# A top-2 FFN's rows loaded seven tiles ahead instead of five, one scatter issued ahead of the last batch's sends, and the last additions of three batches made by Pool

## The chip, the cores and the metric

One core of a Trainium2 chip runs the whole program. The metric is the device time in microseconds (us) of one execution; the runs shown are three, and their median counts. A change of under about 0.5% of this kernel's time (some 10 us) can't be told from none.

## What is computed

Two transformer layers over x of 8 batches x 512 tokens x 128 features, float32. Each layer is an adaLN attention and an adaLN FFN. The change lies wholly in the last of the four, the FFN of layer 1, a mixture of 8 experts of which every token uses two:

```python
xf = x.reshape(B * S, D)                       # D = 128, E = 8 experts, P = 512 hidden
scores = xf @ Wr + br
_, top_idx = jax.lax.top_k(scores, 2)
mask = jax.nn.one_hot(top_idx, E).sum(-2) > 0
router_weights = softmax(where(mask, scores, -inf))
h = gelu(einsum('td,edp->etp', xf, W1) + b1[:, None, :])
y = einsum('etp,epd->etd', h, W2) + b2[:, None, :]
out = einsum('te,etd->td', router_weights, y)
x = x + gb * out
```

## The kernel before

A list of steps (`order.steps`) is written out by hand, and every engine walks the same list, each doing its own share of a step; semaphores tie the shares together. The list ends with the routing of the last batch (b = 7) interleaved with the first seven FFN tiles. After the list each engine has a plain loop for what is left.

**Routing.** For each batch the router chooses two experts a token. DVE works out at which row of a DRAM array `sent` each of the token's two copies goes (`dest`, L2080), and Pool sends them: eight indirect DMAs of 128 rows a batch (step `send`, L2250, semaphore `d_sent`). DVE also makes a list of tiles: tile t2 is 256 rows (`SLOTS`) of one expert. There are 39 tiles (`TILES`). The first 14 (`EARLY`) can be listed before the last batch is routed.

**One tile.** SP loads the expert's weights, a pack of 578 KB (`load_pack`, L1051, three buffers, `PACKS`), and the tile's 256 rows, 132 KB (`load_rows`, L1060, eight buffers `got`, `SENT`). TensorE transposes the rows (`turn2`, L1096), DVE copies them out of PSUM (`rows_T`, L1667), TensorE multiplies up (`up2`), ACT applies gelu (L1500), TensorE multiplies down (`down2`; both at the helper's line L1090), DVE adds the bias (L1675, `y2_drained`) and multiplies by the router weight (L1682, `y2_ready`), and Pool scatters the 256 results to their tokens' rows of the DRAM array `y_rows` with two indirect DMAs (`scatter`, L2134, semaphore `d_y`). TensorE's order in tile t is turn2(t+2), up2(t+1), down2(t).

**SP's order around the change.** SP issues all its DMAs in one order, and a wait holds up what is behind it. Before the loop it loads three packs and `AHEAD` tiles of rows. Then iteration t2 does load_pack(t2+3), which waits until DVE has drained tile t2, and load_rows(t2+`AHEAD`). The latter reads its row number first and then waits for

```python
w.wait_ge(d_y[t2 % SENT], 16 * SLOTS // P * (t2 // SENT))     # L1059
```

that is, until the scatter of the tile eight before has landed, because the scatter reads its destinations from the same `got` buffer. With `AHEAD` = 5 iteration t waits for scatter(t-3).

**Pool's order around the change.** Pool too works in one order: the routing's `stat` of the last batch, scatter(0), (1), (2), (3), (4), the eight sends of the last batch, and then, in its own loop, scatter(5) to (38).

**The end.** When all scatters have landed, SP and ACT load for each batch the two halves of its result into `both` (L1077, L1656, 256 KB each, `d_both`). DVE then does three operations a batch, all 128x512 float32 with both inputs in SBUF: add the halves (L2113), multiply by the gain (L2116), add x (L2119, `out_ready`). SP stores batch after batch, in order of b (L1081), and waits for the stores to land (L1083).

Of the kernel before, what the change touches and what calls it, by code (L numbers as in the profile page):

```python
# [16 lines left out]
ALU = mybir.AluOpType  # L17
# [3 lines left out]
P = 128  # L21
B, S, D = 8, 512, 128
NT = S // P
# [43 lines left out]
TILES_OF = B * S // SLOTS  # L67
ROW = D + 4
PACK = 2 * F + FC + D
PACKS, SENT, AHEAD = 3, 8, 5  # L70


EARLY, FRONT = 14, 7
# [125 lines left out]
def build(nc, t, out):  # L199
    ctx = ExitStack()  # L200
    with ctx:
# [155 lines left out]
        x_tokens = leave([B, NT, D])  # L357
        gain = leave([B, D])
# [31 lines left out]
        both = carve([B, 2, NT, D])  # L390
# [92 lines left out]
        turn_of, back1_of, hrow_of, rank_of, gains_of, fold_of = {}, {}, {}, {}, {}, {}  # L483
# [123 lines left out]
        for b in range(B):  # L607
            n = b * NU
# [281 lines left out]
        def tile(t2):  # L890
            return lambda: add("tile", t2=t2)

        def scatter(t2):
            return lambda: add("scatter", t2=t2)

        for f in (lambda: add("first_tile"), lambda: back1(B - 1), tile(0), lambda: finish1(B - 1), tile(1), tokens_f,
                  stat_f, scatter(0), tile(2), center_f, norm_f, tile(3), router_f, second_f, hrow_f, tile(4), chosen_f,
                  weights_f, scatter(1), scatter(2), tile(5), rank_f, place_f, row_f, scatter(3), scatter(4), tile(6),
                  send_f):
            f()  # L900
        scattered = order.count["scatter"]
# [19 lines left out]
        d_y = [semaphore(f"d_y{z}") for z in range(SENT)]  # L921
        d_both = [semaphore(f"d_both{b}") for b in range(B)]
        tables_ready, row_ready, tiles_ready = (semaphore(n) for n in ("tables_ready", "row_ready", "tiles_ready"))
        turn2_full, got_ready, up2_full, hid2_done, down2_full, y2_drained, y2_ready, out_ready = (
            semaphore(n) for n in ("turn2_full", "got_ready", "up2_full", "hid2_done", "down2_full", "y2_drained",
                                   "y2_ready", "out_ready"))
        meet = semaphore("meet")

        mod_exp, silu_ready, mod_full, mod_ready, consts_ready = (
# [2 lines left out]
        aux_full, aux_drained, pool_done, dve_chain = (  # L932
            semaphore(n) for n in ("aux_full", "aux_drained", "pool_done", "dve_chain"))
# [36 lines left out]
        def drained(s):  # L970

            return s.aux + 1

        with nc.Block() as block:

            @block.sync
            def _(sp):
                w = Waits(sp)
# [13 lines left out]
                for s in order.steps:  # L992
# [19 lines left out]
                    elif s.kind == "copy_out":  # L1012
                        b, a = s["b"], s["a"]
# [3 lines left out]
                    elif s.kind == "parts_out":  # L1017
                        b, what = s["b"], s["what"]
# [4 lines left out]
                    elif s.kind == "stack":  # L1023
                        b, what, r = s["b"], s["what"], s["r"]
# [11 lines left out]
                    elif s.kind == "qload":  # L1036
                        a, q = s["a"], s["q"]
                        b, g = divmod(a, NG)
# [38 lines left out]
                    sp.dma_start(both[:, b, 0, :, :], y_dram[b * S:(b + 1) * S, :].rearrange(  # L1077
                        "(n p) d -> p n d", p=P)).then_inc(d_both[b], 16)
                for b in range(B):
                    w.wait_ge(out_ready, b + 1)  # L1080
                    sp.dma_start(out_v[:, b * NT:(b + 1) * NT, :], both[:, b, 0, :, :]).then_inc(d_out[b], 16)  # L1081
                for b in range(B):
                    sp.wait_ge(d_out[b], 16)  # L1083
# [576 lines left out]
            def _(dve):  # L1660
                w = Waits(dve)
                chain = Chain(w, dve_chain)
# [65 lines left out]
                for s in order.steps:  # L1728
# [13 lines left out]
                    elif k == "mod_first":  # L1742
                        n = SC_A * B
# [4 lines left out]
                    elif k == "mod_signs":  # L1748
                        n = GA_A * B
# [21 lines left out]
                    elif k == "stat":  # L1771
                        L, which, b = s["L"], s["which"], s["b"]
# [12 lines left out]
                    elif k == "center":  # L1785
                        L, which, b = s["L"], s["which"], s["b"]
# [26 lines left out]
                    elif k == "scores":  # L1813
                        u = s["u"]
                        i, n = u["i"], u["n"]
# [6 lines left out]
                    elif k == "maxima":  # L1822
                        n = s["u"]["n"]
# [4 lines left out]
                    elif k == "late":  # L1828
                        n = s["u"]["n"]
                        w.wait_ge(ctx_drained, n + 1)  # L1830
                        dve.reciprocal(ctx_sum[:, 0, n % 2, 2 * P:CW], ctx_sum[:, 0, n % 2, 2 * P:CW]).then_inc(recip, 1)  # L1831
                    elif k == "out_proj":
                        b, i = s["b"], s["i"]
# [4 lines left out]
                    elif k == "router0":  # L1838
                        b = s["b"]
# [65 lines left out]
                    elif k == "before_gather":  # L1905
                        b = s["b"]
# [9 lines left out]
                    elif k == "gather":  # L1916
                        b = s["b"]
# [29 lines left out]
                    elif k == "back" and s["x"] == E - 1:  # L1947
                        b = s["b"]
# [17 lines left out]
                    elif k == "scores1" and s["u"]["i"]:  # L1966
                        u = s["u"]
                        i, n = u["i"], u["n"]
# [139 lines left out]
                for t2 in range(FRONT, TILES):  # L2108
                    tile(t2)
                for b in range(B):  # L2110
                    w.wait_ge(aux_drained, drained(gains_of[b // 4]))
                    w.wait_ge(d_both[b], 32)
                    chain.mark(dve.tensor_tensor(both[:, b, 0, :, :], both[:, b, 0, :, :], both[:, b, 1, :, :],  # L2113
                                                 ALU.add))
                    chain.wait()
                    chain.mark(dve.tensor_tensor(both[:, b, 0, :, :], both[:, b, 0, :, :],  # L2116
                                                 gain[:, b, :].unsqueeze(1).to_broadcast([P, NT, D]), ALU.mult))
                    chain.wait()
                    dve.tensor_tensor(both[:, b, 0, :, :], both[:, b, 0, :, :], x_tokens[:, b, :, :],  # L2119
                                      ALU.add).then_inc(out_ready, 1)  # L2120

            @block.gpsimd
            def _(pool):
# [6 lines left out]
                def scatter(t2):  # L2130
                    z = t2 % SENT
                    w.wait_ge(y2_ready, t2 + 1)
                    for h in range(SLOTS // P):
                        pool.indirect_dma_start(  # L2134
                            y_dram, bass.IndirectOffsetOnAxis(ap=got[:, z, h, D:D + 1].bitcast(U32), axis=0),
                            y_out[:, z, h, :], None, bounds_check=2 * B * S - 1, oob_is_err=False).then_inc(
                                d_y[z], 16)
# [116 lines left out]

                for t2 in range(scattered, TILES):
                    scatter(t2)


# [34 lines left out]
```

## Time and profile before

| what | value |
|---|---|
| three runs | 2068.82, 2073.63, 2080.97 us; median 2073.63 us |
| profiled execution, its own time | 2066.3 us |
| its span | 2064.2 us |
| mean granted TensorE clock | 0.957 |
| TensorE busy | 1803.1 us (87%) |
| DVE / ACT / Pool busy | 1145.4 / 690.3 / 743.9 us |

All times below are microseconds from the start of the span of the profiled execution. The FFN of layer 1 is the stretch from about 1854 to the end; the last batch's routing ends at about 1896, the last tile at 2036, and what is after that is the end described above. "Remote" in a row is a wait whose releaser the profile does not tell. A line of the timeline gives the start, the duration, the engine, line and operation, what it writes and reads, how many instructions are merged, and in brackets the engine's idle time before it with what ended it. SPq rows are DMA issues.

### The profile page before, as it was taken

Reading aid. Unit: us, or ns where it says so; the run is one execution under the profiler, and the core shown is the slowest. Engines: PE = TensorE matmul, PEld = TensorE weight load, DVE = VectorE, ACT = ScalarE, POOL = GpSimd, SP = SyncE. Lnnn points to the kernel's source line nnn. Section 1 sums busy time; section 2 is a strip of 40 time slices with the busy share of each in tenths; the row PEclk is TensorE's granted clock in tenths of the full one; section 3 lists DMA queues with packets and bytes.
Section 4 is the critical chain, followed back from the end, with each engine's and each line's share of the span. In section 5 each row is a group of like instructions: output and inputs, shape, how many; then the busy total and the mean of one; then the engine's idle time right before and its main releaser. Section 6 shows DMA issues by size and latency. Waiting matters only on the chain.

```text
span 2064.2 us, 76401 instructions
## 1 busy us (share of the span) xinstructions
PE 1803.1 (87%) x34864; PEld 1320.1 (64%) x34864; DVE 1145.4 (55%) x2282; ACT 690.3 (33%) x1041; POOL 743.9 (36%) x727
## 2 busy tenths in 40 slices
PE   6899999999888888899999898978888887977994
PEld 4666766766666666575524666766666666756883
DVE  4656666566666665674265555645565545544224
ACT  2333434334333333333101342323333332323431
POOL 2464655555545551311030323313132232014442
PEclk9999999999999999999998999999999989989997
DMA  9500000000000000300012313222131313024666
GB/s 310 164 2 2 2 2 2 2 2 2 2 2 2 2 2 2 103 1 1 3 31 46 82 29 82 52 56 68 38 78 38 73 34 79 20 62 130 198 206 185
DMA packets 81042, 113.45 MB, mean 55 GB/s; under 512 B 9486, under 2 KB 63506, under 8 KB 80289
## 3 DMA queue, kind: packets, MB, share of 16 engines
q1 hardware_dynamic: 71376, 97.16, 17.6%
q0 software_dynamic: 4544, 8.54, 1.2%
q8 instruction: 273, 4.47, 0.9%
q10 hardware_dynamic: 4800, 2.89, 0.6%
q14 instruction: 49, 0.39, 0.1%
HBM read 83.25 MB, written 45.68 MB: 62 GB/s over the span
## 4 chain that ended last, share of the span: by engine, by line
PE 50%; DVE 13%; issue 6%; ACT 2%; DMA 1%; POOL 1%; another core or an unknown queue 1%; POOLq 0%; DVEq 0%; SPq 0%; ACTq 0%
PE psum L1090 47%; DVE colmax L1819 2%; DVE colmax L1972 2%; DVE ctx_sum L1831 1%; PE psum L1438 1%; DVE rowmax L1980 1%; DMA arena<-in_pack 1%; ACT arena L1575 1%; DVE rowmax L1826 1%; DVE arena L1792 1%; DVE stats L1779 1%; DVE raw L1807 1%; PE psum L1165 1%; PE psum L1157 1%
## 5 line engine op out<-in xcount | busy, mean ns | idle before, releaser
L1090 PE MATMUL psum<-arena 128*32 128x32 f32 (+9 forms) x10680 | 679.2, 256 | 84.2 <-issue 56.9
L1090 PEld LDWEIGHTS psum<-arena 128*32 128x32 f32 (+4 forms) x10680 | 489.2, 127 | 205.0 <-issue 128.4
L1575 ACT ACTIVATE arena<-psum 128x1024 f32<-128x1024 f32 (+1 forms) x192 | 169.4, 882 | 359.3 <-PE psum L1090 291.7
L1090 PE MATMUL psum<-prob,ffw 128*32 128x128 f32 x5120 | 206.4, 280 | 40.4 <-DVE rowmax L1826 37.6
L1090 PE MATMUL psum<-neg_ident,rowmax 128*32 128x128 bf16 (+3 forms) x4352 | 215.9, 252 | 11.4 <-issue 10.3
L1972 DVE TENSOR_REDUCE colmax<-psum 128x256 bf16<-128x768 f32 (+2 forms) x160 | 178.3, 1114 | 82.4 <-PE psum L1090 59.3
L1819 DVE TENSOR_REDUCE colmax<-psum 128x512 bf16<-128x2048 f32 (+2 forms) x96 | 168.4, 1755 | 74.7 <-PE psum L1090 74.6
L1980 DVE TENSOR_REDUCE rowmax<-psum 128x2 bf16<-128x256 f32 (+1 forms) x192 | 98.0, 510 | 189.9 <-PE psum L1090 181.3
L1590 ACT COPY ctx_sum<-psum 128x384 f32<-128x384 f32 x128 | 61.2, 478 | 412.4 <-PE psum L1090 366.1
L1090 PEld LDWEIGHTS psum<-prob,ffw 128*32 128x32 f32 x5120 | 139.6, 112 | 71.7 <-DVE rowmax L1826 60.1
L2209 POOL TENSOR_TENSOR arena<-ctx_sum 128x256 f32<-128x256 f32 x128 | 95.4, 745 | 243.9 <-DVE ctx_sum L1831 233.2
L1090 PEld LDWEIGHTS psum<-neg_ident,rowmax 128*32 128x32 bf16 (+1 forms) x4352 | 139.7, 99 | 51.3 <-issue 39.7
L1558 ACT ACTIVATE prob<-psum 128x2048 f32<-128x2048 f32 (+3 forms) x128 | 158.5, 1238 | 29.2 <-PE psum L1090 28.5
L1831 DVE RECIPROCAL ctx_sum<-ctx_sum 128x128 f32<-128x128 f32 x128 | 120.4, 941 | 80.0 <-ACT ctx_sum L1590 79.8
L2158 POOL TENSOR_TENSOR rope_a<-raw,arena 128x512 f32<-128x512 f32 x86 | 110.1, 1280 | 118.8 <-ACT raw L1538 110.6
L2250 POOL DMA_INDIRECT sent<-ffw x64 | 62.6, 978 | 218.4 <-DVE ffw L2087 201.3
L2160 POOL TENSOR_TENSOR rope_b<-raw,arena 128x512 f32<-128x512 f32 x96 | 126.7, 1320 | 37.2 <-ACT raw L1538 29.9
L1090 PE MATMUL psum<-ident_bf,colmax 128*128 128x128 bf16 x1024 | 113.0, 224 | 24.4 <-DVE colmax L1972 17.4
L1090 PEld LDWEIGHTS psum<-ident_bf,colmax 128*128 128x128 bf16 x1024 | 75.5, 100 | 89.4 <-issue 31.1
L2148 POOL TENSOR_SCALAR moments<-moments 128x4 f32<-128x4 f32 x32 | 8.4, 263 | 341.5 <-DVE moments L1783 340.9
L1090 PE MATMUL psum<-prob,ones_col 128*32 128x128 f32 x2560 | 130.8, 277 | 0.0
L1090 PE MATMUL psum<-causal,ident_bf 128*128 128x256 bf16 (+1 forms) x448 | 113.1, 299 | 7.3 <-ACT arena L1575 6.3
(260 smaller groups left out, 2530.3 us busy)
## 6 DMA issues: line engine op xcount, KB each, us to landing
arena<-in_pack SPq DMA_DIRECT2D x39, 578.0 KB
sent<-in_empty SPq DMA_DIRECT2D x9, 2112.0 KB, 34.7
arena<-qk_parts SPq DMA_DIRECT2D x96, 128.0 KB
q_copies<-arena SPq DMA_DIRECT2D x32, 256.0 KB, 3.9
prob<-q_copies SPq DMA_DIRECT2D x128, 64.0 KB, 3.6
qk_parts<-arena SPq DMA_DIRECT2D x16, 384.0 KB, 3.8
arena<-sent SPq DMA_DIRECT2D x39, 132.0 KB
ffw<-in_L_w SPq DMA_DIRECT2D x1, 2048.0 KB, 9.0
```

The costliest lines, as they stand in the source:

```text
L1090: return pe.matmul(o, lhsT, rhs, start=start, stop=stop, skip_group_check=True)
L1558: act.activation(prob_of(u).rearrange("p z j c -> p z (j c)"), scores_of(u).rearrange("p z j c -> p z (j c)"), ACT.Exp, scale=HD0 ** -0.5) ...
L1575: act.activation(probs_of(i)[:, :, h0 * P:(h0 + nh) * P], slot(n)[:, 0:(i + 1) * W].rearrange("p (j c) -> p j c", c=W), ACT.Exp, scale=HD1 ...
L1590: act.copy(ctx_sum[:, 0, n % 2, 0:CW], psum[:, CTX, 0:CW]).then_inc(ctx_drained, 1)
L1819: dve.tensor_reduce(colmax[:, n % 2, :].rearrange("p (z c) -> p z c", z=2), scores_of(u).rearrange("p z j c -> p z c j"), AX.X, ALU.max).t ...
L1831: dve.reciprocal(ctx_sum[:, 0, n % 2, 2 * P:CW], ctx_sum[:, 0, n % 2, 2 * P:CW]).then_inc(recip, 1)
L1972: dve.tensor_reduce(colmax[:, n % 2, 0:W], slot(n)[:, 0:(i + 1) * W].rearrange("p (j c) -> p c j", c=W), AX.X, ALU.max).then_inc(colmax1_d ...
L1980: dve.tensor_reduce(rowmax[:, n % 2, 0:nh], psum[:, MAX, 0:nh * P].rearrange("p (h k) -> p h k", k=P), AX.X, ALU.max).then_inc(max_done, 1)
L2158: chain.mark(pool.tensor_tensor(rope_a[:, z, :], raw[:, z, :], table[:, 0, :], ALU.mult))
L2160: chain.mark(pool.tensor_tensor(rope_b[:, z, :], raw[:, z, :], table[:, 1, :], ALU.mult))
L2209: chain.mark(pool.tensor_tensor(ctxT[b % 2][:, 2 * q:2 * q + 2, i * P:(i + 1) * P], ctx_sum[:, 0, n % 2, 0:2 * P].rearrange("p (c q) -> p ...
L2250: pool.indirect_dma_start(sent, bass.IndirectOffsetOnAxis(ap=dest[:, b % 2, h, n:n + 1], axis=0), sent_row[:, b % 2, h, n, :], None).then_ ...
```

## The change

`AHEAD` becomes 7, the step scatter(5) is put into the list ahead of tile(6) and the last batch's sends, and a new list `BY_POOL` names the batches whose three last operations Pool makes after its last scatter; DVE skips these. `out_ready` becomes two semaphores, and SP waits for the one of the batch's engine.

```diff
-PACKS, SENT, AHEAD = 3, 8, 5
+PACKS, SENT, AHEAD = 3, 8, 7
+BY_POOL = (1, 4, 6)
...
-                  weights_f, scatter(1), scatter(2), tile(5), rank_f, place_f, row_f, scatter(3), scatter(4), tile(6),
+                  weights_f, scatter(1), scatter(2), tile(5), rank_f, place_f, row_f, scatter(3), scatter(4), scatter(5), tile(6),
                   send_f):
...
+        out_ready = [semaphore(n) for n in ("out_by_dve", "out_by_pool")]
...
                 for b in range(B):
-                    w.wait_ge(out_ready, b + 1)
+                    w.wait_ge(out_ready[b in BY_POOL], 1 + sum((c in BY_POOL) == (b in BY_POOL) for c in range(b)))
                     sp.dma_start(out_v[:, b * NT:(b + 1) * NT, :], both[:, b, 0, :, :]).then_inc(d_out[b], 16)
...
                 for b in range(B):                                  # DVE
+                    if b in BY_POOL:
+                        continue
...
                 for t2 in range(scattered, TILES):                  # Pool
                     scatter(t2)
+                for b in BY_POOL:
+                    w.wait_ge(aux_drained, drained(gains_of[b // 4]))
+                    w.wait_ge(d_both[b], 32)
+                    chain.wait()
+                    chain.mark(pool.tensor_tensor(both[:, b, 0, :, :], both[:, b, 0, :, :], both[:, b, 1, :, :],
+                                                  ALU.add))
+                    chain.wait()
+                    chain.mark(pool.tensor_tensor(both[:, b, 0, :, :], both[:, b, 0, :, :],
+                                                  gain[:, b, :].unsqueeze(1).to_broadcast([P, NT, D]), ALU.mult))
+                    chain.wait()
+                    pool.tensor_tensor(both[:, b, 0, :, :], both[:, b, 0, :, :], x_tokens[:, b, :, :],
+                                       ALU.add).then_inc(out_ready[1], 1)
```

## Rows read from the trace of the kernel before

**Rows 1.** Busy time by stretch: busy (instructions) an engine, then TensorE's clock, DMA share, GB/s.
```profile
1950.00:2000.00 50.00, 47.10 (x314) 42.57 (x313) 14.84 (x48) 19.70 (x48) 23.31 (x24) 1.00 0.64 200
2030.00:2064.00 34.00, 4.77 (x38) 4.45 (x36) 17.86 (x30) 1.64 (x4) 5.82 (x6) 0.63 0.71 186
```
**Rows 2.** Chain of waits in order of time, from tile 7 on: start, us, what.
```profile
1897.07 9.88 another core or an unknown queue
...
2025.37 3.80 DMA arena<-in_pack
...
2038.56 2.10 DMA y_rows<-arena
```
**Rows 3.** Timeline, first tiles: SP's issues and TensorE's tile 4.
```profile
1868.12 0.38 SPq L1060 DMA_DIRECT2D arena<-sent  x1
...
1871.80 0.35 SPq L1051 DMA_DIRECT2D arena<-in_pack  x1
...
1880.15 0.35 SPq L1051 DMA_DIRECT2D arena<-in_pack  x1
...
1881.35 3.68 PE L1090 MATMUL psum<-arena 128*128 128x256 f32 x24
```
**Rows 4.** Timeline of Pool, first tiles, the last sends and what follows.
```profile
1872.37 0.98 POOL L2134 DMA_INDIRECT y_rows<-arena  x1 [0.30 <-DVE arena L1682]
...
1892.81 0.96 POOL L2250 DMA_INDIRECT sent<-ffw  x1 [3.78 <-DVE ffw L2087]
...
1902.93 0.99 POOL L2134 DMA_INDIRECT y_rows<-arena  x1 [0.30 <-issue]
```
**Rows 5.** Timeline of DVE, ACT and SP before and in the long wait after tile 7.
```profile
1889.29 0.48 DVE L1682 TENSOR_SCALAR arena<-arena 128x128 f32<-128x128 f32 x2
1891.85 0.17 DVE L2087 TENSOR_SCALAR ffw<-ffw 128x8 uint32<-128x8 f32 x1
...
1906.97 0.42 DVE L1675 TENSOR_TENSOR arena<-psum,arena 128x256 f32<-128x256 f32 x1 [9.91 <-remote]
1912.71 3.11 ACT L1500 ACTIVATE arena<-psum,arena 128x256 f32<-128x256 f32 x8 [13.66 <-remote]
```
**Rows 6.** Timeline of a steady tile: Pool's second scatter, SP's rows.
```profile
1940.22 0.97 POOL L2134 DMA_INDIRECT y_rows<-arena  x1 [0.31 <-issue]
1943.55 0.38 SPq L1060 DMA_DIRECT2D arena<-sent  x1
```
**Rows 7.** Times to landing of the end's loads (L1077), then of its stores (L1081).
```profile
L1077 SPq DMA_DIRECT2D arena<-y_rows x8: 383/562/1796, 2040.8 to 2046.6; - x8
DMA to landing us min/median/max: 3.5/8.3/10.7
...
L1081 SPq DMA_DIRECT2D out<-arena x8: 372/1666/1958, 2048.4 to 2061.4; - x8
DMA to landing us min/median/max: 2.3/6.1/9.6
```
**Rows 8.** Timeline of the end: the first batch and the last operation of DVE.
```profile
2044.82 0.69 DVE L2113 TENSOR_TENSOR arena<-arena 128x512 f32<-128x512 f32 x1 [9.00 <-DMA arena<-y_rows]
2046.88 0.69 DVE L2113 TENSOR_TENSOR arena<-arena 128x512 f32<-128x512 f32 x1
...
2060.65 0.69 DVE L2119 TENSOR_TENSOR arena<-arena,ffw 128x512 f32<-128x512 f32 x1
```
**Rows 9.** Timeline of DVE and Pool near the start: 128x512 operations side by side.
```profile
15.30 0.69 DVE L1801 TENSOR_TENSOR rope_a<-raw,arena 128x512 f32<-128x512 f32 x1 [4.46 <-ACT raw L1538]
15.33 1.78 POOL L2160 TENSOR_TENSOR rope_b<-raw,arena 128x512 f32<-128x512 f32 x1 [8.58 <-ACT raw L1538]
...
17.95 1.26 POOL L2171 TENSOR_TENSOR arena<-rope_a,raw 128x512 f32<-128x512 f32 x1 [0.84 <-DVE raw L1807]
17.98 1.79 DVE L1801 TENSOR_TENSOR rope_a<-raw,arena 128x512 f32<-128x512 f32 x1
```
**Rows 10.** Groups of Pool's instructions: count, busy us, mean ns of one.
```profile
L2174 POOL TENSOR_TENSOR arena<-rope_a,raw 128x512 f32<-128x512 f32 x32 | 40.9, 1278 | 42.4 <-DVE raw L1807 42.0
```

More of the change, by code:

```diff
@@ L923, in build @@
         tables_ready, row_ready, tiles_ready = (semaphore(n) for n in ("tables_ready", "row_ready", "tiles_ready"))
-        turn2_full, got_ready, up2_full, hid2_done, down2_full, y2_drained, y2_ready, out_ready = (
+        turn2_full, got_ready, up2_full, hid2_done, down2_full, y2_drained, y2_ready = (
             semaphore(n) for n in ("turn2_full", "got_ready", "up2_full", "hid2_done", "down2_full", "y2_drained",
-                                   "y2_ready", "out_ready"))
+                                   "y2_ready"))
+        out_ready = [semaphore(n) for n in ("out_by_dve", "out_by_pool")]
         meet = semaphore("meet")
@@ L2119, in _ @@
                     dve.tensor_tensor(both[:, b, 0, :, :], both[:, b, 0, :, :], x_tokens[:, b, :, :],
-                                      ALU.add).then_inc(out_ready, 1)
+                                      ALU.add).then_inc(out_ready[0], 1)
             @block.gpsimd
```

## The prediction

> **What bounds the kernel now.** I read the page's busy shares first (TensorE 87%, so everything before the last tiles is TensorE's), then the busy time by stretch, the chain of waits over the last 200 us, the timelines of SP and Pool, and last the end alone. Nothing of the change acts before about 1847, so only three stretches count.
>
> From 1950 on the tiles run steadily: TensorE is busy 47.10 of 50 us while the DMA engines are at 0.64 [rows 1]; a pack takes 3.80 from issue to landing [rows 2], which with TensorE's 3.7 us a tile makes 4.2 us a tile. In the middle lies a hole. After tile 7, while Pool issues the last batch's eight sends and right behind them the scatters held up by these, the chain stands 9.88 us on something it can't name [rows 2]; DVE waits 9.91 us for TensorE's result of tile 7, and ACT 13.66 [rows 5]. After the last tile, from 2041 on, TensorE has nothing left, and the end belongs to DVE and the DMA engines: DVE's 24 operations take it from 2044.82 to 2061.34 [rows 8], 2.06 us a batch (2046.88 less 2044.82), and the last store lands 2.3 us after its issue [rows 7].
>
> **Rows seven tiles ahead.** No DMA is added; 39 row loads stay, each issued two iterations earlier. What changes is the wait in front of each: iteration t now wants scatter(t-1) landed instead of scatter(t-3). Behind this wait on SP stands the next pack, and TensorE waits for that.
>
> In the steady part: Pool's second scatter of tile 14 is issued at 1940.22, and SP comes to the next row load at 1943.55 [rows 6]. A scatter lands 2.10 us after its last issue [rows 2], here at 1942.3: 1.2 us before it is wanted. Cost nothing; if one lands later, SP has some 2.7 us until the next pack is due, so even a scatter 2 us late is hidden. Nor is there a gain: the chain shows packs, never rows, and TensorE's one wait on SP's loads is for packs.
>
> At the start it is different, because scatter(0) stands behind the routing's `stat` on Pool and its second half is issued only at 1872.37 [rows 4]. SP will come to load_rows(8) at 1868.12 [rows 3] and stand until 1872.37 + 2.10 = 1874.5. Behind it is load_pack(5), which was issued at 1871.80; now it goes at 1874.5 + 1.1 (as SP needs between two issues) = 1875.6, 3.8 us late, and lands 3.80 later, at 1879.4. It is needed by tile 4's up2(5), which starts at 1881.35 [rows 3] for other reasons (the router's steps). Cover left: 1.9 us. load_rows(9) then waits for scatter(1), about 1877, and load_pack(6), due at 1880.15 [rows 3], is not touched. I take 0, bounds 0 and +1.5 (scatters and pack landing 3.4 us later than reckoned, as they share the DMA engines), and not below 0, since nothing comes sooner that anyone waits for. Were the cover gone, the whole 3.8 would show. The two extra loads before the loop find SP idle until 1862. The last two iterations have no row load beside the pack; the last pack without one beside it took the 3.80 that I use, so I give nothing for that.
>
> **One scatter ahead of the sends.** Without it, load_rows(13) in iteration 6 would stand until scatter(5), issued from 1902.93 on [rows 4], had landed; with it, it doesn't. y_out of tile 5 ends at 1889.29 + 0.48 = 1889.77 [rows 5]; Pool sees it 0.8 us later, and two issues of 0.98 with 0.3 between end at 1892.8. The sends were ready at 1892.81 [rows 4] (their destinations and weights done at 1891.85 + 0.17 [rows 5]), and now go at 1893.1: +0.3 us on eight sends. Nobody waits for these but load_rows(14), not due before 1908.
>
> What it does to the hole is the least certain term. The hole lasts as long as Pool issues without a pause: eight sends and scatters 5 and 6, twelve DMAs of 1.27 us, from 1892.81 to 1907.8, and DVE gets TensorE's result at 1906.97 [rows 4, 5]. Now the unbroken run starts with scatter(5) at 1890.5 and ends one pair (2 x 1.27 = 2.5 us) sooner, at 1905.5. If the release follows the run's end, 2.5 us come back at most; if it follows how many issues have gone by since the run began, TensorE is held from its first instruction of tile 7, up to 2.3 us sooner than before, and tile 8 is pushed by up to 2. And even a release at 1904.5 must be followed by pack 10, which is issued when tile 7 is drained and needs 3.80. Bounds -2.5 and +2; I take 0, in the middle, since no row favours an end.
>
> **Pool makes three batches.** This removes nine operations from DVE (9 x 0.69) and puts nine on Pool. What counts is whether the two engines can work side by side. The rows of the start show the same two shapes: Pool's 128x512 with two SBUF inputs takes 1.26 to 1.28 alone [rows 9, 10]; started 0.03 behind a DVE operation of the same kind it takes 1.78, and a DVE operation started 0.03 behind Pool's takes 1.79 instead of 0.69 [rows 9]. So they run one after the other: a pair costs 17.98 + 1.79 - 17.95 = 1.82 us whoever is first, instead of 1.27 side by side.
>
> Work out the end with that. DVE does b = 0 alone until 2046.96. Half of `both` for b = 1 is in by then, and from there on Pool has nine operations and DVE twelve: nine pairs x 1.82 = 16.4, three of DVE alone x 0.685 = 2.05, together 18.4, so 2046.96 + 18.4 = 2065.4 against 2061.34: +4.1 us. Data doesn't hold this up much: the last load is issued at 2046.6 and lands within 10.7, at 2057.3 [rows 7], while the pairs are still behind. The last store then follows as before (2.3 us).
>
> Bounds: with no interference at all, Pool would do b = 1, 4, 6 by about 2060.4 and DVE end at 2059.5, but the stores also have to drain: they were issued from 2048.4 on and the first landed 9.6 us later [rows 7], at 2058, since loads at a DMA share of 0.71 over the whole stretch [rows 1] go first; eight stores from there leave little. So -0.5 at best. At worst Pool's operations cost 10% more with a broadcast gain, and Pool's chain lags: +6. I take +4.1, by the row of the same shape.
>
> The Trainium skill, "SBUF — State Buffer", section "SBUF: two separate sides", speaks against this part: a DVE instruction with two SBUF inputs and a Pool instruction that reads SBUF take one shared port pair as an exclusive lock, the first for the whole instruction, and the other fully blocks. By that rule nothing of an operation overlaps: 9 x 1.27 + 12 x 0.69 = 19.7 from 2046.96, an end at 2066.7, +5.4. The rows show a pair at 1.82 where the rule would have 1.96, so a little does overlap; the measured pair decides.
>
> **Sum.** On the profiled execution: 2066.3 + 0 (rows) + 0 (hole) + 4.1 (end) = 2070.4. The median of the three runs is 7.3 above the profiled one, a spread of the executions that the change doesn't touch, so 2073.63 + 4.1 = 2077.7.
>
> **Rivals.**
> 1. Faster: the hole closes. Place: between tile 7 and tile 9; price: the pair that leaves the unbroken run, -2.5, and the end gains its -0.5 because the stores' draining sets it: 2073.63 - 3 = 2070.6 (2063.3 on the profiled one). For it: DVE's release at 1906.97 falls at the last of the run's issues. Against: the pair of [rows 9] for the end, pack 10 for the hole. It decides if Pool's operations of the end show 1.27 beside DVE's.
> 2. SP's new wait bites. load_rows(8) is released late, pack 5 lands after 1881.35, tile 4 waits 1.5, and the router's steps of the last batch, which stand behind tile 4, with it; the sooner throttled tile 7 adds 2. 2073.63 + 4.1 + 3.5 = 2081.2. For it: the cover is a mere 1.9 us in a stretch where packs, rows and scatters meet. Against: all of it must be late together.
> 3. The change of engines is hidden: the pairs cost 1.82, but the stores' draining and the loads' landing set the end (the b = 7 loads land at 2057.3 and three operations and eight stores follow), so that only +1 is seen: 2074.6. Against: DVE's pairs are 8 us behind the last landing.
>
> **Chances.** Forecast 0.55, rival 1 0.18, rival 2 0.15, rival 3 0.12. The terms together run from -3 to +9.5, thus 2070.6 to 2083.1; the three runs lie from 4.8 below to 7.4 above their median, and half of that goes on either end: 2068 to 2086. Slower by over 0.5% (10.4 us) needs rival 2 with all bounds and a high draw: 0.11. Faster by over 0.5% needs more than any term holds: 0.05. The rest, 0.84, is within 0.5%, which is about what a measurement of this kernel can tell from no change.
>
> **What would show it.** In the end stretch: Pool's nine operations at about 1.8 and DVE's mostly at 1.2 to 1.8 instead of 0.69, the last DVE operation near 2065. On SP: load_rows(8) at about 1874.5 and load_pack(5) at 1875.6, with tile 4 starting when it did. On Pool: scatter(5) at 1890.5, sends from 1893.1. In the hole: tile 7 drained at 1905 to 1909. Wrong would be: operations of 0.69 and 1.27 side by side (then the end gains), a TensorE wait for pack 5, or tile 7 drained before 1903.

## The result, and the profile after

Eighteen runs of each kernel, taken in turn: before 2069.57 us median (2060.61 to 2081.59), changed 2076.12 us (2070.28 to 2085.57), ratio 1.0034 with a 95% interval of 1.0017 to 1.0050. So the change costs 7 us (3.5 to 10.3), or 0.34%: little, but with eighteen runs of each the interval lies clear of 1. 2077.7 had been forecast from a median of 2073.63, that is +4.1.

The profiled execution of the changed kernel took 2085.57 us (span 2083.8), 19 us more than that of before. That is no measure of the change: DVE takes the FFN's tile 0 out of PSUM at 1874.1 instead of 1861.8, and in a second profile of the same changed kernel at 1864.5. All comparisons below are therefore of stretches, measured from that point ("+13.0" is 13.0 us after it; the tiles in the table are counted at the same operation of theirs) or from the first operation of the end.

| stretch, us | before | changed | changed, second profile |
|---|---|---|---|
| tile 0 to tile 6 | 34.0 | 35.0 | 37.5 |
| tile 6 to 7 | 11.15 | 10.77 | 8.74 |
| tile 7 to 9 | 10.2 | 11.3 | 8.2 |
| tile 0 to the last tile | 173.0 | 174.2 | 173.5 |
| end: DVE's first operation to its last | 16.52 | 19.60 | 19.61 |
| end: DVE's first operation to the program's end | 19.34 | 25.25 | 25.26 |

The middle moved by about 1 us, which is no more than two executions differ by: from tile 0 to the last took 175.4 in an experiment below ("One batch on Pool") whose middle is that of before. The end is 5.9 us longer in both profiles.

First the steady part and the end by stretches (columns as in [rows 1]): TensorE 47.67 us of 50, DMA share 0.65, as before; in the end Pool is now as busy as DVE.

```profile
1965.00:2015.00 50.00, 47.67 (x315) 42.88 (x315) 14.88 (x48) 19.70 (x48) 23.31 (x24) 1.00 0.65 199
2045.00:2083.80 38.80, 3.34 (x30) 3.15 (x29) 19.19 (x21) 0.65 (x2) 19.35 (x15) 0.61 0.62 163
```

The end on DVE, timeline, to be held against [rows 8]. L2118, L2121 and L2124 are the three operations of a batch:

```profile
2058.51 0.69 DVE L2118 TENSOR_TENSOR arena<-arena 128x512 f32<-128x512 f32 x1 [9.11 <-DMA arena<-y_rows]
...
2062.62 1.05 DVE L2118 TENSOR_TENSOR arena<-arena 128x512 f32<-128x512 f32 x1 [1.96 <-DMA arena<-y_rows]
...
2068.36 1.63 DVE L2124 TENSOR_TENSOR arena<-arena,ffw 128x512 f32<-128x512 f32 x1
2069.92 1.74 DVE L2118 TENSOR_TENSOR arena<-arena 128x512 f32<-128x512 f32 x1
2071.70 1.63 DVE L2121 TENSOR_TENSOR arena<-arena,ffw 128x512 f32<-128x512 f32 x1
2073.36 1.63 DVE L2124 TENSOR_TENSOR arena<-arena,ffw 128x512 f32<-128x512 f32 x1
2074.92 1.74 DVE L2118 TENSOR_TENSOR arena<-arena 128x512 f32<-128x512 f32 x1
2076.70 0.69 DVE L2121 TENSOR_TENSOR arena<-arena,ffw 128x512 f32<-128x512 f32 x1
2077.42 0.69 DVE L2124 TENSOR_TENSOR arena<-arena,ffw 128x512 f32<-128x512 f32 x1
```

And the same stretch on Pool:

```profile
2061.85 1.26 POOL L2269 TENSOR_TENSOR arena<-arena,ffw 128x512 f32<-128x512 f32 x1
...
2069.53 1.59 POOL L2272 TENSOR_TENSOR arena<-arena,ffw 128x512 f32<-128x512 f32 x1
2071.08 1.70 POOL L2266 TENSOR_TENSOR arena<-arena 128x512 f32<-128x512 f32 x1
...
2074.53 1.59 POOL L2272 TENSOR_TENSOR arena<-arena,ffw 128x512 f32<-128x512 f32 x1
```

Where Pool is idle, DVE's operation takes 0.69; beside Pool's it takes 1.63 to 1.74, and Pool's 1.59 instead of 1.26. From 2069.92 to 2074.92 three pairs pass: 1.67 us a pair. Of DVE's last twelve operations seven are such full pairs. This is the turn-taking of [rows 9]. DVE's sum: nine operations fewer, -6.2 (9 x 0.685); waiting for batch 2's data, to which it comes sooner since it skips batch 1, +2.0, so that the three operations of batch 1 (2.06) are no gain at all; its last twelve operations in 15.5 us (2062.62 to 2078.11) instead of 8.2, +7.3. Together +3.1.

The other 2.8 us are not on DVE. The last store is issued at 2078.14 and lands 2.3 us later, at 2080.4; the program should end at 2080.7. It ends at 2083.8. What stands there is on the line that closes the program, where each engine waits for its own work to come to an end (DRAIN). The rows of that line, of the changed kernel (engine, operation, duration in ns, start in us):

```profile
L977 POOLq DRAIN  x1: 8740/8740/8740, 2074.5 to 2074.5; - x1
L977 DVEq DRAIN  x1: 725/725/725, 2077.4 to 2077.4; - x1
...
L977 SPq DRAIN  x1: 13/13/13, 2080.7 to 2080.7; - x1
L977 SPq EVENT_SEMAPHORE  x1: 17/17/17, 2083.7 to 2083.7; - x1
```

and of the kernel before:

```profile
L974 POOLq DRAIN  x1: 9740/9740/9740, 2036.9 to 2036.9; - x1
...
L974 SPq DRAIN  x1: 13/13/13, 2063.9 to 2063.9; - x1
```

Pool's closing wait lasts until 7.1 us after Pool's last operation: 2074.5 + 8.74 = 2083.2 against 2076.12 now, 2036.9 + 9.74 = 2046.6 against 2039.5 before. Before, it was over 17 us ahead of SP. Now Pool's last operation comes 4.3 us before the last store lands, and SP, done at 2080.7, stands 3.0 us for it.

The start of the FFN, on SP (L1063 rows, L1054 pack), to be held against [rows 3]:

```profile
1887.09 0.38 SPq L1063 DMA_DIRECT2D arena<-sent  x1
1888.23 0.35 SPq L1054 DMA_DIRECT2D arena<-in_pack  x1
```

and on TensorE, tile 4:

```profile
1893.56 3.68 PE L1093 MATMUL psum<-arena 128*128 128x256 f32 x24
```

load_rows(8) stands until scatter(0) has landed, at +13.0, and pack 5 is issued at +14.1 (12.7 and 13.8 were forecast). Tile 4 starts at +19.5, as in [rows 3] (1881.35 less 1861.8 is 19.55): hidden.

On Pool, scatter(5), the first send, and scatters 6 and 7, to be held against [rows 4]:

```profile
1902.77 0.97 POOL L2139 DMA_INDIRECT y_rows<-arena  x1 [1.54 <-DVE arena L1685]
...
1905.33 0.96 POOL L2255 DMA_INDIRECT sent<-ffw  x1 [0.30 <-issue]
...
1916.80 0.99 POOL L2139 DMA_INDIRECT y_rows<-arena  x1 [0.30 <-issue]
1921.61 0.97 POOL L2139 DMA_INDIRECT y_rows<-arena  x1 [3.82 <-DVE arena L1685]
```

Scatter(5) goes at +28.7 and the first send at +31.2, both as forecast. The unbroken run now ends at 1917.8 (+43.7), not at +46.0 as in [rows 4]. And the hole is still there; chain of waits, then DVE's row, to be held against [rows 2] and [rows 5]:

```profile
1911.30 8.57 another core or an unknown queue
1919.89 0.43 DVE arena L1678
1920.49 3.84 DMA arena<-in_pack
```

```profile
1919.89 0.42 DVE L1678 TENSOR_TENSOR arena<-psum,arena 128x256 f32<-128x256 f32 x1 [8.20 <-remote]
```

Tile 7 is released at +45.8 (before +45.2), though the run ended 2.3 us sooner. In the six profiles that have the hole the release comes anywhere from 0.8 us before the run's end (the kernel before) to 2.3 us after it, and 2.2 after it in "One batch on Pool", whose scatters and sends stand as before; so it does not follow the run's end. Behind it pack 10 takes its 3.84.

### The profile page after: what moved, and what is told of

It reads as the page before. It is cut to its first block, busy times and chain, and to the rows that moved or that the text cites. A ratio compares the mean times of both kernels' runs of the same rounds, so it can differ in the third digit from the quotient of the medians.

```text
span 2083.8 us, 76402 instructions
## 1 busy us (share of the span) xinstructions
PE 1814.8 (87%) x34864; PEld 1329.9 (64%) x34864; DVE 1146.1 (55%) x2273; ACT 690.5 (33%) x1041; POOL 757.8 (36%) x736
## 4 chain that ended last, share of the span: by engine, by line
PE 49%; DVE 14%; issue 7%; DMA 2%; ACT 2%; POOL 1%; another core or an unknown queue 1%; SPq 0%; ACTq 0%; DVEq 0%; POOLq 0%
PE psum L1093 47%; DVE colmax L1975 2%; DVE colmax L1822 2%; DMA arena<-in_pack 1%; DVE ctx_sum L1834 1%; PE psum L1441 1%; DVE rowmax L1983 1%; DVE raw L1810 1%; ACT arena L1578 1%; DVE rowmax L1829 1%; DVE arena L1795 1%; PE psum L1168 1%; ACT prob L1561 1%; PE psum L1160 1%
## 5 line engine op out<-in xcount | busy, mean ns | idle before, releaser
L1093 PE MATMUL psum<-prob,ffw 128*32 128x128 f32 x5120 | 211.9, 285 | 39.9 <-DVE rowmax L1829 37.3
L1093 PEld LDWEIGHTS psum<-prob,ffw 128*32 128x32 f32 x5120 | 143.8, 114 | 71.9 <-DVE rowmax L1829 59.5
L1561 ACT ACTIVATE prob<-psum 128x2048 f32<-128x2048 f32 (+3 forms) x128 | 158.5, 1238 | 28.7 <-PE psum L1093 28.1
L1093 PE MATMUL psum<-ident_bf,colmax 128*128 128x128 bf16 x1024 | 112.9, 223 | 28.1 <-DVE colmax L1975 19.5
```

Of the source, the lines that this page charges most:

```text
L1093: return pe.matmul(o, lhsT, rhs, start=start, stop=stop, skip_group_check=True)
L1561: act.activation(prob_of(u).rearrange("p z j c -> p z (j c)"), scores_of(u).rearrange("p z j c -> p z (j c)"), ACT.Exp, scale=HD0 ** -0.5) ...
```

## The experiments

Theory A, after this reading: the end costs +3.1 by turn-taking and +2.8 by Pool's closing wait, and the middle nothing. Rivals: the closing wait is only a symptom of the end (B); SP's new wait costs something in the middle (C).

The kernels below were timed in three sets, each beside its own runs of before. In set 1 (the end alone, the middle alone, something late on Pool, Pool busy) before took 1992.31 us (23 runs, 1985.94 to 2002.4); in set 3 (rows six ahead again, the first two batches, the two with scatters held) 1995.83 us (29 runs, 1985.46 to 2009.89). No profile of these two sets has the hole, and the mean granted clock is about 0.97. Set 2 (the whole again, rows alone, rows six ahead, one batch) was like the forecast's runs: before 2070.78 us (19 runs, 2065.29 to 2082.4), clock 0.955, and the hole in every profile. The expectations speak of a chip with or without the hole. But the chip number noted with set 1 is 10, and with sets 2 and 3 it is 13 both times; so whether the hole goes with the chip or with something that changes in time is open, and only "a set with the hole" and "a set without" can be said. This matters more than most edits.

**The end alone.** The changed kernel with the two middle edits undone.

```diff
-PACKS, SENT, AHEAD = 3, 8, 7
+PACKS, SENT, AHEAD = 3, 8, 5
...
-                  ..., scatter(3), scatter(4), scatter(5), tile(6),
+                  ..., scatter(3), scatter(4), tile(6),
```

> Only the end of the change: Pool makes the last operations of batches 1, 4 and 6; rows five tiles ahead and the scatters as before. The end stretch is read from DVE's first operation of the end to the end of the span: 19.4 us in the kernel before, 25.3 in the changed one. Theory (the end alone makes the kernel slower, in two parts: DVE and Pool take turns, 3.1 us, and Pool's closing drain outlasts all else by 2.9): 25.3 again, a median 5 to 7 us above before. Rival (the middle makes half of it): the end stretch is 25.3 too, as a profile shows it, but the median only some 3 us above before.

Measured: 2000.63 us (12 runs), ratio 1.0038 (1.0021 to 1.0056), that is +7.6 us (4.2 to 11.2), where 5 to 7 were expected. DVE's end 19.60 and end stretch 25.25, to 0.01 those of the changed kernel. So the end alone is enough for the loss of the changed kernel.

**The middle alone.** The kernel before with the two middle edits.

```diff
-PACKS, SENT, AHEAD = 3, 8, 5
+PACKS, SENT, AHEAD = 3, 8, 7
...
-                  ..., scatter(3), scatter(4), tile(6),
+                  ..., scatter(3), scatter(4), scatter(5), tile(6),
```

> Only the middle of the change: rows seven tiles ahead and scatter(5) ahead of the last sends; DVE makes all of the end. The middle is read from tile 0's drain to tile 38's (DVE's bias additions): 173.0 us before, 174.3 in the changed kernel. Theory: 173 to 174.5, end stretch 19.4, a median within 2 us of before. Rival (the middle costs the measured surplus over the predicted 4.1): a median 3 or more above before. Rival from the prediction (the hole closes): 170.5 or less, a median below before.

Measured: 1998.48 us (12 runs), ratio 1.0029 (1.0011 to 1.0046), +5.8 us (2.2 to 9.2), where 2 at most was expected. The rival's "3 or more" came, but from a place that neither had named. End stretch 19.34, the old one. SP's timeline:

```profile
1832.20 0.35 SPq L1051 DMA_DIRECT2D arena<-in_pack  x1
1838.58 0.38 SPq L1060 DMA_DIRECT2D arena<-sent  x1
1839.72 0.35 SPq L1051 DMA_DIRECT2D arena<-in_pack  x1
```

Pool's, from the last send to scatter(6):

```profile
1833.59 0.96 POOL L2250 DMA_INDIRECT sent<-ffw  x1 [0.30 <-issue]
1834.86 0.99 POOL L2134 DMA_INDIRECT y_rows<-arena  x1 [0.30 <-issue]
1836.15 0.99 POOL L2134 DMA_INDIRECT y_rows<-arena  x1 [0.30 <-issue]
```

and TensorE's:

```profile
1843.64 5.28 PE L1090 MATMUL psum<-arena 128*128 128x256 f32 x24 [3.22 <-DMA arena<-in_pack]
```

load_rows(14) wants scatter(6), whose issues stand behind all eight sends and end at 1837.1. Until 1838.58 SP stands; pack 11, due at about 1836.1 (tile 8 is drained at 1835.5), goes only at 1839.72, and TensorE waits 3.22 for it. Tile 9 to 10 takes 8.72 us; in the kernels of sets 1 and 3 without this wait it takes 3.7 to 4.2. The 4.6 to 5.0 us more are the wait and a slower block behind it (5.28 instead of 3.78 us, at a granted clock of 0.76 from 1843 to 1850). From tile 0 to the last 167.9 us pass, in those others 161.7 to 164.0. Theory C holds here, at another load than the one that I had watched. Where the hole is, load_rows(14) comes late anyway, because the hole keeps SP back, and the same wait is free.

**Something late on Pool.** The kernel before; Pool's last operation is a memset of 128x4 after DVE's last.

```diff
                 for t2 in range(scattered, TILES):
                     scatter(t2)
+                w.wait_ge(out_ready, B)
+                pool.memset(minus_half[:, :], -0.5)
```

> The kernel before, with one tiny memset (128x4) on Pool that waits until DVE has made its last operation; nothing else is changed, and no operation of Pool's stands beside DVE's. Theory (Pool's closing drain ends 7.1 us after Pool's last operation, whatever that is, and is hidden only while Pool finishes early): the end stretch grows from 19.4 to about 24 us (last DVE operation 16.5 after the first, the memset, 7.1, half a microsecond). Rival (the drain of the changed kernel took long because of the big operations or of the port): it stays within 0.5 us of 19.4.

Measured: 2002.33 us (one run), DVE's end 16.57, end stretch 24.06 against 19.3. Pool's timeline and the closing line:

```profile
1992.89 0.10 POOL L2258 MEMSET minus_half<- 128x4 f32 x1 [21.84 <-DVE arena L2119]
```

```profile
L974 POOLq DRAIN  x1: 7220/7220/7220, 1992.9 to 1992.9; - x1
...
L974 SPq DRAIN  x1: 13/13/13, 1995.4 to 1995.4; - x1
```

One operation of 0.10 us, put late on Pool, costs 4.7 us: SP is done at 1995.4 and the program ends at 2000.3. B would have the stretch stay at 19.3; it is out.

**Pool busy without SBUF inputs.** The kernel before; Pool makes three memsets of 128x1024 for each of three batches in place of operations that read.

```diff
+                for b in (1, 4, 6):
+                    w.wait_ge(d_both[b], 32)
+                    for _ in range(3):
+                        chain.wait()
+                        chain.mark(pool.memset(rope_a[:, :, :].rearrange("p z c -> p (z c)"), 0.0))
```

> The kernel before, with nine memsets of 128x1024 on Pool into a dead buffer, three each when the data of batches 1, 4 and 6 have landed; they write SBUF and read none of it. DVE still makes all 24 operations. Theory (the turns are taken over the read side that a two-input DVE operation and a reading Pool operation share): DVE's operations stay at 0.69 us and its 24 end 16.5 us after the first, end stretch 19.4. Rival (any work of Pool's in SBUF holds DVE up): DVE operations beside a memset take 1 us or more, and the 24 end 19 us or later after the first.

Measured: 1995.85 us (one run). DVE's operations keep their 0.69 beside Pool's 2.97 us of memsets a batch, and its end is 16.66 (16.5 before). So that Pool is busy in SBUF is not enough to make DVE wait. That it is Pool's reading which does it fits this, but a memset differs from an addition in more than that, and no run puts another kind of reading operation on Pool there. The end stretch is 21.68, where 19.4 was expected, since Pool's last memset comes late and the closing wait with it:

```profile
1983.71 2.97 POOL L2261 MEMSET rope_a<- 128x1024 f32 x3 [0.64 <-DMA arena<-y_rows]
```

```profile
L974 POOLq DRAIN  x1: 8083/8083/8083, 1985.7 to 1985.7; - x1
```

(1985.7 + 8.08 = 1993.8, 7.1 after 1986.7.)

**The whole change again**, as it stands in the diff, in set 2.

> The changed kernel itself, once more. Between tile 7 and tile 9 the profile before has a hole of some 9 us in which TensorE's results reach nobody (tile 7 drained 11.2 us after tile 6, tile 8 another 5.9), and the profiles of the experiment with the end alone have none (4.2 and 4.6). Theory (SP's new wait costs what the hole does not hide): where a run has no hole, load_rows(14) stands until scatter(6) has landed, 3 us or more, pack 11 is that late, and the whole costs 10 to 13 us; where it has the hole, load_rows(14) waits for nothing and the whole costs 6 to 7. Rival (the middle costs a fixed share, whatever the hole does): the same loss either way.

Measured: 2075.05 us (10 runs), ratio 1.0019 (0.9999 to 1.0040), +3.9 (-0.2 to 8.3). Its profile is the last column of the table: the end is the same to 0.01, the middle within 0.5 us of before. The interval includes 1, so by itself this timing neither repeats the loss nor contradicts it. The other half of the expectation, 10 to 13 us where there is no hole, was not tested: the whole change never ran in such a set. The two parts measured alone in set 1, +7.6 and +5.8, would add up to 13 if neither hides the other.

**Rows alone**, without the moved scatter.

```diff
-PACKS, SENT, AHEAD = 3, 8, 5
+PACKS, SENT, AHEAD = 3, 8, 7
```

> Rows seven tiles ahead and nothing else; scatter(5) stays behind the last batch's sends. Theory: SP stands one iteration earlier, load_rows(13) until scatter(5) has landed, some 12.5 us after the first send, and packs 10 and 11 are late: tile 0's drain to tile 38's at least 3 us longer than with the scatter ahead (167.9 there), where the run has no hole. Rival (the scatter ahead buys nothing): the same 167.9 within 1.

Measured: 2072.57 us (one run). SP in the hole:

```profile
1911.89 0.38 SPq L1060 DMA_DIRECT2D arena<-sent  x1
1915.18 0.00 SPq L1051 DMA_DIRECT2D arena<-in_pack  x1
```

load_rows(13) now stands until scatter(5), behind the sends, has landed (+45.0), and pack 10 goes at +48.3, 2.2 us later after tile 7's drain (+45.5) than in the other kernels (0.6). From tile 7 to 9 11.8 us pass, from tile 0 to the last 173.9; the changed kernel has 11.3 and 174.2, so nothing is seen of the scatter here. The expectation, 3 us more without it, was for a set without the hole and stays untested: what the moved scatter is worth no run shows. SP was free again at +46.1, so its wait for the scatter alone does not account for the pack at +48.3.

**Rows six ahead**, with the moved scatter and the old end.

```diff
-PACKS, SENT, AHEAD = 3, 8, 5
+PACKS, SENT, AHEAD = 3, 8, 6
...
-                  ..., scatter(3), scatter(4), tile(6),
+                  ..., scatter(3), scatter(4), scatter(5), tile(6),
```

> The middle of the change with rows six tiles ahead instead of seven; scatter(5) ahead of the sends; DVE makes all of the end. Iteration t then waits for scatter(t-2). Theory (it is the wait of iteration 7 for scatter(6), which stands behind the eight sends on Pool): load_rows(14) now is issued in iteration 8, pack 11 goes within 0.7 us after tile 8's drain, and tile 0's drain to tile 38's is within 1.5 us of the 161.7 to 163.4 of a middle left as it was. Rival (the scatter ahead of the sends, or any rows loaded early, costs the 4 to 6 us): 166 or more again.

Measured: 2067.03 us (10 runs), ratio 0.9983 (0.9960 to 1.0005). Pack 11 goes 0.6 us after tile 8's drain, as expected, but the 161.7 to 163.4 of the expectation are of a set without the hole, and this set has it: 174.3 us from tile 0 to the last, against 173.0 before, 174.2 in the changed kernel and 175.4 with one batch on Pool. So the profile shows no gain in the middle.

> The version with rows six tiles ahead and the one scatter more, and the old end: timed once more, in more rounds, whether it is below the kernel before at all. From its first timing 0.998 (0.996 to 1.0005). If the one tile less takes SP's wait out of packs' way on every chip, 0.998 to 1.000; if the steps gained there were chance, 1.000 +- 0.001. On a chip without the hole, rows_six waits for scatter(6) one iteration later than rows seven ahead, so tile 9 to 10 keeps its 4.2 us instead of 8.7.

Measured again, in set 3, without the hole: 1991.77 us (12 runs) against 1995.83, ratio 0.9987 (0.9967 to 1.0008). Pack 11 again goes 0.6 us after tile 8's drain, tile 9 to 10 takes 3.74, and tile 0 to the last 162.2, so one iteration less ahead takes SP's wait out of the pack's way. Both intervals hold 1: this version lies below the kernel before in both sets, and is not shown to be faster.

**One batch on Pool**, b = 1 alone, with the middle of before.

```diff
-BY_POOL = (1, 4, 6)
+BY_POOL = (1,)
```

> Pool makes the last operations of batch 1 alone; everything else as before. Pool is done by some 7 us after DVE's first operation of the end, so its 7.1 us of closing drain are over 5 us before the stores. Theory (two separate prices: taking turns about 1.0 a batch, the drain only if Pool finishes last): DVE's operations take 17.3 to 17.6 us from the first to the end of the last, end stretch 20.1 to 20.4. Rival (the whole surplus of 5.9 is in proportion to the batches): 21.3. Rival (one batch less on DVE is a gain when the drain is hidden): below 19.3.

Measured: 2073.35 us (one run). DVE's end 17.85 (+1.3), end stretch 20.66; both lie 0.25 above what was expected. Pool's closing wait starts at 2055.2 and lasts 8.74, over at 2063.9, 7 us before SP is done: hidden. DVE comes to batch 2 before its data:

```profile
2054.78 0.97 DVE L2118 TENSOR_TENSOR arena<-arena 128x512 f32<-128x512 f32 x1 [2.06 <-DMA arena<-y_rows]
2055.78 1.63 DVE L2121 TENSOR_TENSOR arena<-arena,ffw 128x512 f32<-128x512 f32 x1
```

Three operations fewer save 2.06, this wait takes the 2.06 back, and the two lengthened operations add 1.2: that is the +1.3.

**The first two batches on Pool**, with the middle of before.

```diff
-BY_POOL = (1, 4, 6)
+BY_POOL = (0, 1)
```

> The kernel before with the first two batches of the end made by Pool instead of three spread ones. Two parts of the end are told apart. If the engines take turns (a pair 1.67 us), DVE's eighteen operations and Pool's six make 6 x 1.67 + 12 x 0.69 = 18.3 us for the end's additions, +1.8 over the 16.5 of before; and since Pool's last operation then ends some 7 us before DVE's, its closing wait (7.1 us after its last operation) is hidden: end stretch 18.3 + 2.9 = 21.2, +1.9 in all, ratio 1.0009. If the closing wait instead hangs on the program's end and not on Pool's last operation, the stretch is 24 to 25. If only the number of batches mattered, two of the changed kernel's three would cost 2/3 of +5.9, that is +3.9 (stretch 23.2).

Measured: 2001.15 us (10 runs), ratio 1.0009 (0.9983 to 1.0036). The line that closes the program:

```profile
L977 POOLq DRAIN  x1: 8742/8742/8742, 1987.1 to 1987.1; - x1
...
L977 SPq DRAIN  x1: 13/13/13, 2001.5 to 2001.5; - x1
```

The closing wait is over at 1995.8, 5.7 us before SP, whose end now follows DVE's last operation (1998.9) by the usual 2.8. Measured from the first operation of the end, which is Pool's at 1979.76, the additions take 19.15 and the stretch 21.9; 18.3 and 21.2 were expected, without DVE's wait until batch 2's data are in at 1983.42. By then all but the last 0.3 us of Pool's first three operations are over, so the full pairs are three and not six. Six operations on Pool, and no closing cost: it hangs on when Pool's last operation comes, not on their number nor on the program's end. The medians lie 5.3 us apart, but the interval holds 1, and the profile has 2.6 us of it.

**Scatters 5 and 6 held until tile 7 is weighted**, in the kernel before, to see whether the hole's end follows the end of Pool's run.

```diff
-                    w.wait_ge(y2_ready, t2 + 1)
+                    w.wait_ge(y2_ready, 8 if t2 in (5, 6) else t2 + 1)
```

> The kernel before, with scatters 5 and 6 waiting until DVE has weighted tile 7, so that Pool's unbroken run is the eight sends alone (8 x 1.27 = 10.1 us instead of 15). Where the hole between tiles 7 and 9 exists (span above 2050): if the late news of TensorE's work is released when Pool's run ends, DVE gets tile 7 some 4 to 5 us sooner than the 1906.97 of before (measured from tile 0: 40 to 41 instead of 45.1), tile 9 follows sooner by as much, and the time falls by 3 to 5 us, ratio 0.998. If it is released by something that doesn't depend on the run's end (TensorE's clock, the DMA engines' load), tile 7 stays at 45 after tile 0 and the ratio is 1.000 +- 0.001. On a chip without the hole (about 1992) both expect 1.000. The end is the old one: DVE 16.5 us, end stretch 19.3.

Measured: 1994.07 us (10 runs), ratio 0.9995 (0.9973 to 1.0017), in a set without the hole, where both theories had 1.000. It tells nothing about the hole.

**The same with rows six ahead and the moved scatter.**

> Rows loaded six tiles ahead, scatter(5) ahead of the last batch's sends and waiting, as scatter 6, until tile 7 is weighted: this puts scatter(5)'s wait in front of the sends, so the eight sends go only after tile 7. If the hole is made by the sends' unbroken run, tile 7 itself is drained without it (on a chip with the hole: 6 to 7 takes 4 to 5 us instead of 11), and the stall moves behind it, to tiles 8 and 9, where the batch's destinations are wanted much later; the stretch from tile 0 to the last tile then stays at 172 to 175. If the hole belongs to tile 7 for another reason (its clock), 6 to 7 stays at 10 to 11.

Measured: 2008.3 us (one run), 12 us above the median of before, though runs of before in this set reach 2009.89; what counts is the profile. Having no hole, it answers another question, what SP's wait costs at its worst. Pool's last send and scatter(6):

```profile
1851.34 0.96 POOL L2250 DMA_INDIRECT sent<-ffw  x1 [0.30 <-issue]
1852.60 0.98 POOL L2134 DMA_INDIRECT y_rows<-arena  x1 [0.30 <-issue]
1853.89 0.99 POOL L2134 DMA_INDIRECT y_rows<-arena  x1 [0.30 <-issue]
```

SP:

```profile
1844.77 0.35 SPq L1051 DMA_DIRECT2D arena<-in_pack  x1
1856.32 0.38 SPq L1060 DMA_DIRECT2D arena<-sent  x1
1857.46 0.35 SPq L1051 DMA_DIRECT2D arena<-in_pack  x1
```

and TensorE:

```profile
1849.54 5.46 PE L1090 MATMUL psum<-arena 128*128 128x256 f32 x24 [3.02 <-DMA arena<-in_pack]
...
1861.52 6.35 PE L1090 MATMUL psum<-arena 128*128 128x256 f32 x24 [6.30 <-DMA arena<-in_pack]
```

load_rows(14) stands until scatter(6) has landed, and pack 12 behind it, due at about 1846.9 (tile 9 is drained at 1846.3), goes at 1857.46, 10.6 us late. Pack 11 is late too, by 1.6 us, behind load_rows(13) and the held scatter(5). TensorE waits 3.02 and 6.30 for the two and afterwards runs blocks of 3.8 us in 5.46 and 6.35, at a granted clock of 0.68 from 1850 to 1855 and 0.77 from 1855 to 1870. Tile 0 to the last takes 173.8 against 162 to 164.

## Why the prediction was right, step by step

**Rows, 0: right, with its times to 0.3 us.** load_rows(8) at +13.0, pack 5 at +14.1, tile 4 untouched. But the sentence that nobody waits for the sends "but load_rows(14), not due before 1908" held only where the hole is, for 1908 is the hole's doing. Without it SP comes there about 5 us before scatter(6) has landed, and "the middle alone" lost 5.8 us. Rival 2 had the mechanism right, at the wrong load. That the forecast's 0 came true is luck in this: the changed kernel was timed where the hole hides the wait.

**The hole, 0: right in size, and its cause stays open.** The run ended 2.3 us sooner and tile 7's release was at +45.8 instead of +45.2, 46.2 in the second profile, so the guess that would have gained, release at the run's end, failed. The other guess, a release up to 2.3 us sooner or a tile 8 pushed by 2, is neither shown nor out: with the middle of before the release came at +45.2 in one profile and at +47.5 in another (one batch on Pool). The experiment made for this ran in a set without the hole.

**The end, +4.1: right mechanism, a pair mis-sized, and a second cost missed.** The turn-taking came as reckoned, at 1.67 us a pair instead of 1.82, and DVE's chain lengthened by 3.1 instead of 4.1. A wait of 2.0 for batch 2's data was not in the working ("data doesn't hold this up much"), and of the nine full pairs, which were, there were seven. With a broadcast gain Pool's operation did not get dearer. What failed is "the last store then follows as before (2.3 us)": it does, but the program does not end with it. Pool's closing wait adds 2.8 as soon as Pool's last operation comes less than about 7 us before the last store has landed. Together +5.9. The range's worst was +6, but for other reasons (Pool's operations 10% dearer, its chain behind), so that the range covers the closing wait is luck; no term stood for it. Two mis-sized terms, 1.0 too much and 2.8 too little, came to a sum 1.8 off.

The Trainium skill, "SBUF — State Buffer", section "SBUF: two separate sides", would have whichever of the two starts first hold the shared ports for its whole instruction and the other fully block. By that rule an estimate from the rows' durations is 0.69 + 1.26 = 1.95 a pair. The rows have 1.67: nearly so, but 0.28 us of a pair do overlap. That memsets on Pool leave DVE at 0.69 is what the same rule, which speaks of a Pool instruction that reads SBUF, would have.

**Sum.** 0 + 0 + 5.9 from the profiles, against 6.6 us between the medians, or 7 (3.5 to 10.3) by the ratio. Rival 1's price for the end (-0.5) and rival 3's (+1) are both excluded by end stretches of 25.25 and 25.26.

## What to carry to other kernels

Before work is moved to a second engine at the end of a program, look at three things: whether rows of the same shape show the two engines side by side or in turns, whether the data are there when the first engine comes to its next piece sooner, and how long after its last operation each engine's closing wait ends. In these runs Pool's last operation had to come 7 us before the last store lands. A load issued further ahead waits for a younger event; look where the order of the other queue puts a long run in front of that event, and do not trust a due time that a stall in the profile has made. And time a change in more than one set of runs, each beside its own runs of before, if the profile holds a stall that it can't name.

## What the runs showed of the hardware

- Pool's closing wait ends 7.1 us after the end of Pool's last operation, be it a scatter's issue (2039.5 to 2046.6), an addition (2076.1 to 2083.2), or a memset of 0.10 us (1993.0 to 2000.1). In the changed kernel DVE's takes 0.73 us, over 0.05 after its last operation, and ACT's 0.16.
- The same kernel takes 2070 us at a mean granted clock of 0.955, with a hole of some 10 us after tile 7, in one set of runs, and 1992 to 1996 us at 0.97 without one in two others. Already tile 0 comes at 1862 in the one and at about 1800 in the others, so some 60 of the 75 to 78 us lie ahead of the FFN. The profile of before and that of the held scatters 5 and 6, the same program up to there, are within 5 us of each other until 1245, counted at the same instruction of ACT; from 1300 to 1700, with the hole, TensorE is granted 0.95, 0.95, 0.95 and 0.91 in the four hundreds of us, without it 0.98, 1.00, 0.98 and 0.95. Why, and whether it goes with the chip, no run here shows.
- The hole's cause stays open. It is an unnamed wait of 8.57 us in the changed kernel and 9.88 in the kernel before. The same ten to twelve issues of Pool at the same 1.27 us stand there in the sets without it, so they alone do not make it; whether they take part where it is was not settled.
